# The last feed-forward layer by dispatch: tokens scattered to expert blocks in HBM, 23 blocks of 128 rows, results scattered to the output

## The reference

```
router_probs = softmax(x @ Wr)                      # x: 2048 x 128, Wr: 128 x 8
expert_idx   = argmax(router_probs);  p_max = max(router_probs)
outs[e]      = gelu(x @ W1[e] + b1[e]) @ W2[e] + b2[e]     # 128 -> 512 -> 128, for e = 0..7
out          = p_max * outs[expert_idx]
x            = x + tanh(g_ffn[3]) * out             # x inside the part is layernormed
```

## Time and profile before

| what | us |
|---|---|
| median of 3 runs (1240.64 to 1251.58) | 1242.35 |
| the profiled execution's own time | 1250.19 |
| its span on the core | 1248.4 |
| busy in the span: PE / PE weight loads | 1123.4 (90%) / 865.4 |
| busy: DVE / ACT / POOL | 627.1 / 554.1 / 258.2 |

### The profile page before, as it was taken

How to read it: one execution, slowest core, us unless ns; L and a number is a source line. 1 busy time by engine, 2 the same in 40 slices (tenths; PEclk the granted TensorE clock), 3 DMA queues, 4 the chain that set the end, 5 groups by cost and what they waited for, 6 DMA issues and landing times.

```text
span 1248.4 us, 18922 instructions
## 1 busy us (share of the span) xinstructions
PE 1123.4 (90%) x6802; PEld 865.4 (69%) x6802; DVE 627.1 (50%) x1869; ACT 554.1 (44%) x1283; POOL 258.2 (21%) x287
## 2 busy tenths in 40 slices
PE   1899888845989989898989999999999999999998
PEld 0677676633657766566677878888887878777766
DVE  0555675757764464635673756555565332222212
ACT  1456454401233343323545565555555565444342
POOL 3334453400001121302031312123223010000000
PEclk9989998856997799888999999999999999999999
DMA  8000000000000000000000100000100000000000
GB/s 306 1 1 2 2 1 1 1 0 1 1 1 1 1 1 1 1 1 2 1 2 1 49 21 1 1 1 1 69 1 1 2 1 1 9 1 9 1 9 9
DMA packets 6781, 16.01 MB, mean 13 GB/s; under 512 B 1433, under 2 KB 4129, under 8 KB 6306
## 3 DMA queue, kind: packets, MB, share of 16 engines
q1 hardware_dynamic: 6690, 14.80, 3.3%
HBM read 13.73 MB, written 1.05 MB: 12 GB/s over the span
## 4 chain that ended last, share of the span: by engine, by line
PE 80%; DVE 12%; ACT 3%; issue 3%; SPq 2%; DMA 1%; POOL 1%; DVEq 0%; ACTq 0%
PE BK L508 25%; PE SP L615 10%; PE BK L764 9%; PE BK L660 7%; PE BK L570 4%; PE BK L532 4%; PE BK L635 3%; PE BK L631 3%; DVE X L1285 3%; PE BK L741 2%; PE SP L598 2%; PE BK L540 2%; PE BK L503 2%; PE SP L602 1%; PE BK L573 1%
## 5 line engine op out<-in xcount | busy, mean ns | idle before, releaser
L1109 DVE TENSOR_REDUCE mx<-SP 128x8 f32<-128x616 f32 x112 | 89.4, 798 | 119.5 <-PE SP L615 117.2
L508 PEld LDWEIGHTS BK<-R,hT 128*128 128x128 f32 x1152 | 134.5, 192 | 14.7 <-issue 11.7
L508 PE MATMUL BK<-R,hT 128*128 128x128 f32 x1152 | 137.3, 276 | 0.0
L615 PE MATMUL SP<-kT,qT 128*128 128x308 f32 (+1 forms) x512 | 132.1, 394 | 0.0
L1285 DVE SCALAR_TENSOR_TENSOR X<-BK,wsel,X 128x128 f32<-128x128 f32 x128 | 36.1, 344 | 178.0 <-PE BK L508 135.9
L968 ACT ACTIVATE hT<-BK,cols_s 128x512 f32<-128x512 f32 x128 | 85.1, 688 | 71.4 <-PE BK L764 68.9
L764 PE MATMUL BK<-xT,R 128*128 128x512 f32 x256 | 115.3, 594 | 0.0
L1369 POOL TENSOR_SCALAR vv<-mv 128x2 f32<-128x2 f32 (+1 forms) x52 | 11.9, 228 | 453.1 <-DVE mv L1036 453.0
L615 PEld LDWEIGHTS SP<-kT,qT 128*128 128x128 f32 x512 | 84.9, 202 | 27.0 <-issue 18.0
L1439 POOL TENSOR_TENSOR P<-P,rec 128x616 f32<-128x616 f32 x48 | 58.4, 1217 | 208.8 <-DVE rec L1131 208.8
L660 PE MATMUL BK<-PT,V 128*128 128x128 f32 x768 | 97.8, 282 | 4.1 <-ACT PT L931 4.1
(11 more groups left out here) (198 smaller groups left out, 1887.9 us busy)
## 6 DMA issues: line engine op xcount, KB each, us to landing
R<-in_f3w SPq DMA_DIRECT2D x2, 2048.0 KB, 7.5
w_s<-in_w SPq DMA_DIRECT2D x1, 1536.0 KB, 12.6
R<-in_f0w SPq DMA_DIRECT2D x2, 512.0 KB, 8.7
out_x<-X SPq DMA_DIRECT2D x4, 256.0 KB, 2.3
X<-in_x SPq DMA_DIRECT2D x1, 896.0 KB, 7.3
ctxT_s<-in_ctxT SPq DMA_DIRECT2D x1, 616.0 KB, 5.1
R<-in_mask SPq DMA_DIRECT2D x1, 616.0 KB, 8.1
R<-in_fside SPq DMA_DIRECT2D x1, 616.0 KB, 9.6
```

The source lines that it names most:

```text
L508: m = e.matmul(o, a, b, start=(i == 0), stop=(i == n - 1), skip_group_check=True)
L615: m = e.matmul(o, lhs, rhs, start=(l == 2 and j % 2 == 0), stop=True, skip_group_check=True)
L1109: e.tensor_reduce(mb, sv, AXX, ALU.max, negate=True).then_inc(s_max, 1)
```

## The change

Every token is computed for its own expert only. The tokens' rows are written to a table `disp` in HBM, at rows that belong to their experts, read back in blocks of 128 rows, computed, and written to the output by token number.

- A row of the table is 258 numbers: the layernormed token (128), the token before the layernorm (128), its gate `p_max * tanh(g)`, and its number. `ST` on the chip holds the rows of all 16 tiles. Expert `e` owns rows from `2048 e` on. At the start of the kernel 11 DMAs fill all 18304 rows with a pad row whose number lies outside the output (18.9 MB by their size).
- `F3` now ends after routing in two new stages. `slots`: five bfloat16 matmuls count, for each token, how many tokens of its expert come before it. `send`: POOL scatters the four tiles of the group, with one indirect DMA for each tile (16 in all).
- A new item `M` follows the last group. `blocks` makes a list of 15 further blocks from the experts' counts. Then come 23 blocks: number 0 to 7 is the first 128 rows of each expert, with weights loaded as before (`W1E`, `W2E`); number 8 to 22 are the listed ones, with weights fetched for each from HBM into one of three buffers `WD`. All 23 are always computed. Block `k` does `bT` (transpose), `bup` (four matmuls of 128 columns), `bdown` (four of 128 columns); step `s` of the plan holds `bT s`, `bup s-1`, `bdown s-2`, in this order.
- ScalarE applies Gelu in four 128-column instructions a block. VectorE copies the transposed tile, adds the bias, and applies gate and residual. POOL scatters each block to the output by an indirect DMA that skips pad rows.
- `down3`, `wT`, `bias3` and `store` are gone. `w2`, `w2o`, `f2w1` move into one buffer `R3` that `ST` reuses; `XB` (8 row buffers) lies over `qT`, `WD` over `V`.

```
 # schedule
     if kind == "F3":
+        return ["stats", None, "apply", "lnT", "route3a", "route3b", "slots", "send"]
+    if kind == "M":
+        steps = [[(name, k - lag) for lag, name in ((0, "bT"), (1, "bup"), (2, "bdown")) if 0 <= k - lag < NBLK]
+                 for k in range(NBLK + 2)]
+        return [("blocks",)] + steps
 # TensorE
+                elif kind == "bT":
+                    k = item[0]
+                    i, f = take(stage)
+                    e.wait_ge(d_row[k % 8], 16 * (k // 8 + 1))
+                    e.transpose(BK[:, i, 0:128], XB[:, k % 8, 0:128], ident).then_inc(f, 1)
+                elif kind == "bup":
...
+                    else:
+                        e.wait_ge(d_expert[(k - NFIX) % 3], 32 * ((k - NFIX) // 3 + 1))
+                        w = WD[:, (k - NFIX) % 3, 0:512]
+                    e.wait_ge(*emptied(("bT", k)))
+                    for j in range(4):
+                        m = e.matmul(BK[:, i, 128 * j:128 * j + 128], w[:, 128 * j:128 * j + 128], xTb[:, k % 2, :],
+                                     start=True, stop=True, skip_group_check=True)
...
+                elif kind == "bdown":
...
+                    e.wait_ge(*emptied(("bup", k)))
+                    mms(BK[:, i, 0:128], [(hTb[:, k % 2, j, :], w[:, 128 * j:128 * j + 128]) for j in range(4)]).then_inc(
+                        f, 1)
 # VectorE, bdown
+                    e.wait_ge(*full(stage))
+                    if k > 3:
+                        e.wait_ge(*put(k - 4))
+                    e.tensor_tensor(OB[:, k % 4, :], BK[:, i, 0:128], B2E[:, k, :] if k < NFIX else b2d[:, (k - NFIX) % 3, :],
+                                    ALU.add).then_inc(o, 1)
+                    e.wait_ge(*emptied(stage))
+                    e.scalar_tensor_tensor(OB[:, k % 4, :], OB[:, k % 4, :], XB[:, k % 8, 256:257], XB[:, k % 8, 128:256],
+                                           ALU.mult, ALU.add).then_inc(s_done, 1)
 # POOL
+                elif kind == "send":
...
+                    e.wait_ge(s_slot, g + 1)
+                    for t in range(4 * g, 4 * g + 4):
+                        e.indirect_dma_start(disp[:, :], bass.IndirectOffsetOnAxis(ap=slot[:, t:t + 1], axis=0), ST[:, t, :],
+                                             None).then_inc(d["sent"], 16)
+                elif kind == "bdown":
+                    e.wait_ge(s_done, k + 1)
+                    e.indirect_dma_start(out[:, :], bass.IndirectOffsetOnAxis(ap=XBid[:, k % 8, ROW - 1:ROW], axis=0),
+                                         OB[:, k % 4, :], None, bounds_check=NB * 128 - 1, oob_is_err=False).then_inc(
+                                             d_put[k % 4], 16)
 # SP
+                elif kind == "blocks":
+                    e.wait_ge(d["sent"], 16 * NB)
+                    for k in range(NFIX):
+                        e.dma_start(XB[:, k, :], disp[FULL * k:FULL * k + 128, :]).then_inc(d_row[k], 16)
+                    e.wait_ge(s_list, 1)
+                    for k in range(NFIX, NBLK):
+                        i, s = k - NFIX, (k - NFIX) % 3
+                        row = e.value_load(bi[0:1, 0, i:i + 1], min_val=0, max_val=NROW - 128)
+                        ex = e.value_load(bi[0:1, 1, i:i + 1], min_val=0, max_val=7)
+                        if i > 2:
+                            e.wait_ge(*emptied(("bdown", k - 3)))
+                        e.dma_start(WD[:, s, :], I["f3p"][bass.DynSlice(ex, 1), :, :].rearrange("e p f -> p (e f)")).then_inc(
+                            d_expert[s], 16)
+                        e.dma_start(b2d[:, s, :], I["b2e"][bass.DynSlice(ex, 1), :].broadcast_to([128, 128])).then_inc(
+                            d_expert[s], 16)
+                        e.wait_ge(*put(k - 8))
+                        e.dma_start(XB[:, k % 8, :], disp[bass.DynSlice(row, 128), :]).then_inc(d_row[k % 8], 16)
```

More of the change, by code:

```diff
@@ L30 @@
 NROWS = 128 * 23
[L32 to L36, removed]
+KF_ID, KF_HM, KF_VM, KF_TRI, KF_IOTA, KF_MH, KF_J, KF_I, KF_E = 0, 128, 144, 152, 216, 224, 228, 243, 258
+NKF = 266
+KB_ID, KB_NEG, KB_ONE, KB_SEL, KB_M8, KB_T8, KB_LT, KB_EB = 0, 128, 512, 640, 1256, 1384, 1512, 1640
+NKB = 1648
+ROW = 258
+FULL = 2048
+NFIX, NDYN = 8, 15
+NBLK = NFIX + NDYN
+NROW = 8 * FULL + 128 * NDYN
+OUTSIDE = 1 << 20
+NPAD = 11
+WROW = 1028
 INS = [
@@ L145, in ready @@
         if kind == "F3":
-            g = item[1]
-            return all(ended(("A", 3, 4 * g + i, 0), t) for i in range(4)) and (g == 0 or begun(("F3", g - 1), 8, t))
+            return all(ended(("A", 3, 4 * item[1] + i, 0), t) for i in range(4))
+        if kind == "M":
+            return all(ended(("F3", g), t + 1) for g in range(4))
+        if kind == "ids":
+            return all(ended(("F2", g), t) for g in range(4))
         if kind == "load3a":
@@ L197, in bank_uses @@
             "up0": [1] * 4, "down0": [1] * 4, "up1": [1] * 4, "down1": [1], "up2": [1] * 4, "down2": [1],
-            "up3": [1] * 4, "down3": [1], "wT": [1], "bias3": [1]}.get(kind, [])
+            "slots": [1], "blocks": [1], "bT": [1], "bup": [1], "bdown": [1]}.get(kind, [])
 class Tables:
@@ L233, in __init__ @@
         xn2 = [s for s in self.plan if s[0] == "apply" and s[1] == "P"]
-        xn4 = [s for s in self.plan if s[0] == "apply" and s[1] != "P"]
+        xn4 = [s for s in self.plan if s[0] == "apply" and s[1] not in ("P", "F3")]
         ups = []
@@ L778, in tensor_program @@
                     i, f = take(stage)
[L779 to L791, removed]
+                    w = W2E[:, k, :] if k < NFIX else WD[:, (k - NFIX) % 3, 512:1024]
@@ L987, in scalar_program @@
                         e.wait_ge(s_end2, g - 1)
+                    once(d["pad"], 16 * NPAD)
                     e.copy(o16[:, g % 2, :, :].rearrange("p a n -> p (a n)"), BK[:, i, :]).then_inc(o, 1)
-                elif kind == "wT":
+                elif kind == "bup":
+                    k = item[0]
                     i, _, o, _ = bank_of(stage)
-                    if item[0]:
-                        e.wait_ge(*full(("bias3", item[0] - 1)))
                     e.wait_ge(*full(stage))
-                    e.copy(wT[:], BK[0:8, i, :]).then_inc(o, 1)
+                    if k > 1:
+                        e.wait_ge(*full(("bdown", k - 2)))
+                    for j in range(4):
+                        c = C_L3FB1 + 4 * k + j
+                        b = cols[:, c:c + 1] if k < NFIX else WD[:, (k - NFIX) % 3, 1024 + j:1025 + j]
+                        m = e.activation(hTb[:, k % 2, j, :], BK[:, i, 128 * j:128 * j + 128], ACT.Gelu, bias=b)
+                    m.then_inc(o, 1)
         def vector_program(e):
@@ L1272, in vector_program @@
                     e.wait_ge(*emptied(stage, 1))
-                elif kind in ("down0", "down3"):
+                elif kind == "down0":
                     g, part = item
-                    if kind == "down3":
-                        e.wait_ge(s_wsel, g + 1)
-                    for u in range(len(bank_uses(stage))):
-                        ex = part if kind == "down3" else 4 * part + u
-                        w = wsel if kind == "down3" else ksel
+                    for u in range(4):
+                        ex = 4 * part + u
                         i, _, o, _ = bank_of(stage, u)
@@ L1476, in build @@
+            for k in range(NBLK - 4, NBLK):
+                e.wait_ge(*put(k))
         block = ctx.enter_context(nc.Block())
```

248 lines of the change are left out of this document (181 added, 67 removed).

## The result

| | before | changed |
|---|---|---|
| median, us | 1241.49 (4 runs, 1235.17 to 1251.58) | 1184.59 (4 runs, 1175.94 to 1197.56) |
| profiled execution / its span | 1250.19 / 1248.4 | 1175.94 / 1174.1 |
| PE busy | 1123.4 (90%) | 963.7 (82%) |

The ratio is 0.951 (95% interval 0.941 to 0.961). The forecast was 1175 with a range of 1130 to 1235. A second set of four runs of the same changed kernel in a later session gave 1195.23 and a ratio of 0.948 (0.939 to 0.956).

A forecast was written before the change was run, and what follows sets the result against it. TensorE was taken to bound the kernel before. Attention 55 us earlier, then uncovered routing, block steps and end put the span at 1181 against 1248.4; 1242.35 - 67.5 = 1175 us, range 1130 to 1235.

The forecast's parts named there:

- attention's last addition, from the mark: Attention ends 55 us earlier; the mark is SP's issue of the last weight load of the third layer.
- from there to the first `bT`: After attention: the last group's uncovered routing, four scatters, their landing and reading back a block, 23.1 us.
- steps 0 to 10: Start of the block loop: two steps at half clock, nine at full, one table load, 27 us.
- a round of steps 11 to 22: Listed blocks with fetched weights: 8.65 us a step, twelve steps 104 us.
- DMA part: In each of steps 11 to 22: fetching 722 KB, 4.1 us plus 0.4 for issues, 4.5 us.
- end: After the last step: `bup 22`, two `bdown` at half clock, DVE, last scatter and its landing, 9.5 us.
- POOL's cost of one indirect DMA: Each scatter on POOL: 1.2 us, between 0.37 and 4.5, with no trace row showing one.
- closed round trip: Steps 11 to 22: `bT s` waits for rows released by step `s-1`, so three buffers hide nothing; 8.65 us a step.
- second case: Rival for steps 11 to 22: TensorE at full clock, 6.9 us a step, 1147 us in all; chance 0.15.
- clock's rule: TensorE in sparse stretches: throttled is the default and activity releases it, speaking for half clock; no size given.
- Attention's end: Last attention units: 7 us of idle TensorE, 4.8 of it from group 1's scatters ahead of POOL's scaling.
- pads: Kernel's opening: 18.9 MB of pad rows written behind the loads, 55 us of DMA, costed at nothing.

The follow-up runs named there:

- experiment 1: Changed kernel with five weight buffers instead of three: 1128.34 us, 2.85 us a block.
- experiment 2: Changed kernel, three buffers, with the rows of block k+1 issued behind the weights of block k: 1113.75 us, 3.86 us a block.
- experiment 3: Changed kernel with a block's rows issued first, its weights and bias behind them: 1149.55 us, 6.49 us a block.
- experiment 5: Changed kernel with 18 unused matmuls on TensorE ahead of each `bT` from block 11 on: 1163.94 us, 7.08 us a block.
- experiment 7: Changed kernel with group 1's four scatters three steps later in the plan: 1164.68 us.
- experiment 8: Kernel before plus only the 11 pad DMAs: 1248.36 us (10 runs), ratio to the kernel before 0.999.
- experiment 9: Changed kernel with five weight buffers, the bias packed behind the weights and group 1's scatters late: 1099.21 us (4 runs), ratio to the kernel before 0.878.

## Why the prediction was right

The step of the argument that decided was the reading of the loop. Term by term, in the profiled execution:

| term | forecast | measured |
|---|---|---|
| attention's last addition, from the mark | -55 | 121.8 - 175.0 = -53.2 |
| from there to the first `bT` | 23.1 | 23.2 |
| steps 0 to 10 | 27 | 23.2 |
| a round of steps 11 to 22 | 8.65 | 8.79 |
| of it TensorE / DMA part / DVE | 3.8 / 4.5 / 0.35 | 3.9 / 4.39 / 0.46 |
| end | 9.5 | 9.8 |
| mark to end | -67.5 | -67.6 |
| POOL's cost of one indirect DMA | 1.2 | 0.96 busy, 1.26 apart |

(175.0 is the end of the addition and 121.8 its start, because the forecast has the 0.35 us of the addition in the next term; from start to start it is -52.9.)

The agreement of the sum to 0.1 us is luck. It is made of an attention 1.7 us later than forecast, first steps 3.8 shorter and rounds 1.5 longer in all, and the changed kernel's second profile has 64.9 less than before instead of 67.6.

- **The closed round trip** was right in its place, its order and its size. Experiments 1 to 3 each open it in another way. The third takes away just what its link weighed, 2.10 us of the DMA part; the first two let one trip serve four blocks and two, and their periods are 2.85 and 3.86.
- **The DMA part.** Two landings of the earlier trace rows and a line between them gave 4.5; it took 4.39. The Trainium skill, "DMA: Bandwidth & Descriptors", section "Anatomy of one DMA", gives a fixed 2.0 us and the bytes at 436 GB/s, an estimated 3.7 for the 722 KB of a round (thousands of bytes; the trace's units make it 514 + 64 + 129 = 707). Trace and page differ by 0.7: the page's rule is for one DMA and counts no time between issues, and here the last of the three is issued 1.04 behind the first; from that one it is 3.35. For the 129 KB of the rows alone the page gives an estimated 2.3, and experiment 3 measured 2.29, although SP issued this DMA and the page fitted GpSimd's.
- **The clock.** The second case (full clock, 1147) was wrong for this kernel: 0.61 in the window of the rounds. Experiment 5 put its price at 17 to 19 us where the prediction said 28. The 28 was 1.75 a round, right against 1.71, or 21 over the twelve; the other 7 lay in the steps behind the routing and in the end, ahead of which this filler does not stand.
- **The clock's rule.** TensorE's clock fell to 0.55 in the routing, where it was 22% busy, stayed at 0.61 in the rounds, and was 1.00 in those of experiment 5, where only the waits had been filled. The busy share by itself doesn't order the cases: over the twelve rounds experiment 2 has 0.93 at 61% and experiment 3 has 0.58 at 59%, and a pass at the lower clock is itself longer. The Trainium skill, "TensorE: Matmul & The Clock Gate", section "Part 1: The HAM clock gate (the "warmup" mystery)", says that activity releases the throttle; the trace agrees, from both sides.
- **Attention's end.** 7 us of idle time were charged, between nothing and 20. The attention ended 1.7 later than forecast. The place was right (POOL's scaling behind the scatters, a wait of 3.05), but in experiment 7 its removal brought 1.9 against the same profile; behind it stands the chain of copies of the last unit.
- **Steps 0 to 10** were over-priced by 3.8, and two errors hide in it. The prediction counted eleven full steps, but step 0 has only a transpose and step 1 only a transpose and a `bup`: at half clock the two took 2.75 us and not 7.6. Step 2 was at half clock too (3.63), step 3 took 2.02, and steps 4 to 9 ran at 1.90 instead of 2.05. The table load of 1.28 came at 1024.42, in the routing, where ACT had nothing to do. And the scatter eight blocks back, "long landed" in the prediction, was not: SP stood at the landings of blocks 0 and 1 before it could issue the rows of blocks 8 and 9, the rows of block 10 came late behind them, and TensorE waited 1.11 at its `bT`. From the chain of waits:

```profile
1045.71 4.44 DMA out_x<-hT,qT
...
1050.31 0.33 SPq L1643
...
1053.01 3.52 DMA qT<-disp
```

- **The pads**: nothing, as said. But the working was off: at the 345 GB/s of the earlier trace rows they would take 55 us, and at the 234 to 241 GB/s of the six profiles they take about 79, to 109 us. There were over 800 us of cover, so it didn't matter.
- **POOL** is no hindrance in the block loop: its scatter of 0.98 us fits into a 1.90 us step. Only the landing of the first two was, as told above.

**The 9.6 us between 1175 and the median** are not a term of the sum. The profiled run, 1175.94, is the fastest of its four, with its mark 6.7 us earlier than in the profile of before; the others' spans, less the 283.5 behind the mark, put their marks at an estimated 895 to 912. Over both sets of runs the medians differ by 56.9 and 60.8, the traces behind the mark by 67.6. Whether these 7 to 11 us lie ahead of the mark by chance or by the change stays open: the pads alone cost nothing there (experiment 8), and experiment 9, whose dispatch kernel does the same work up to the mark, has it at 891.2. The range of the prediction came from terms of the change alone and left this out; it held because it was wide for other reasons.

## What to carry to other kernels

When buffers are fetched ahead, follow one fetch around the loop: which release starts it, which engine's order stands between its landing and the next release. If the first instruction of step `s` waits for a fetch that step `s-1` releases, the number of buffers is no depth at all, and the period is the sum of all links; put what is needed first ahead in the issue order (2.3 us a round here), or issue it a step earlier (4.9), or add buffers (5.9, and the trip then spans several blocks but is still closed). And a stretch where no engine is half busy pays a second time through TensorE's clock, 1.7 of 8.8 us a round here.

## What the runs showed of the hardware

- An indirect DMA of 128 rows, on POOL: 0.96 to 1.0 us busy, the next 1.26 behind it, and the scatters of a block landed 3.4 us after their issue (median of 23; those to the table 2.7, median of 16), against 2.3 for a plain store of 256 KB.
- Two register loads and three DMA issues take SP 2.69 us (experiment 1); the issues are 0.52 apart, so the loads are an estimated 0.57 each, (2.69 - 3 x 0.52) / 2; in the changed kernel's chain of waits the two start 0.57 apart. Hidden in the slow loop, they are a link of the fast one.
- Writes of 1032-byte rows from one small tile ran at 234 to 241 GB/s; the opening loads at 345.
- 514 KB (fetched at a row chosen by a register) landed in 3.2 us, an estimated 164 GB/s for one such fetch; with the fetches of several blocks overlapping, 265 were reached.
- The column of the granted clock is not to be trusted in the opening. In the kernel before it says 1.00 in the first 40 us (the earlier trace rows have it too), yet eight passes there take 2.08 us, where the same line takes 1.16 later. That is near the ratio of the two levels (1.9 to 2.0 and 1.06 for eight passes in the changed kernel's steps at half and at full clock):

```profile
12.80 2.08 PE L570 MATMUL BK<-R,oT 128*128 128x128 f32 x8 [3.56 <-ACT oT L893]
...
401.62 1.16 PE L570 MATMUL BK<-R,oT 128*128 128x128 f32 x8 [1.33 <-ACT oT L893]
```
